# A transformer block on one NeuronCore: Q and K halves spilled head by head, each stack filled by one transfer

## What is computed

```python
x = x + attention(layernorm(x))     # x: 4 x 512 x 512, f32
x = x + ffn(layernorm(x))
# attention: 16 heads of 32, causal, softmax(q k^T / sqrt(32)) v, then @ Wo
# ffn: w1, w3 (1365 x 512) and w2 (512 x 1365), each rounded to -s, 0, +s
#      with s = mean |w|;  (silu(x w1^T) * (x w3^T)) w2^T
```

## Time and profile before

| | us |
|---|---|
| median of 3 runs | 585.4 |
| lowest and highest | 580.27, 587.4 |
| the profiled execution | 582.54 |
| its span in the profile | 580.8 |
| TensorE busy in that span | 544.1 (94%) |
| VectorE, GpSimd, ScalarE busy | 374.1, 290.1, 265.1 |

### The profile page before, as it was taken

The page is one execution under the profiler, slowest core; times in us unless marked ns, Lnnn a source line. Parts: engine busy times, 40 slices in busy tenths (PEclk is TensorE's granted clock), DMA queues, the critical chain, the costliest instruction groups (busy, mean ns, idle before and its releaser), DMA issues.

```text
span 580.8 us, 8895 instructions
## 1 busy us (share of the span) xinstructions
PE 544.1 (94%) x3148; PEld 250.3 (43%) x3148; DVE 374.1 (64%) x937; ACT 265.1 (46%) x437; POOL 290.1 (50%) x339
## 2 busy tenths in 40 slices
PE   3788888899879999999999999999989999999997
PEld 2343333344434444444444444444434444444443
DVE  7887787585998747545797666653865854554421
ACT  4867678656443455243244544422236654013320
POOL 5170598792763574811706662731537779113320
PEclk9898789999989999999999999999989999999999
DMA  8988848957563212203664003005430001150001
GB/s 323 322 173 236 211 113 230 232 148 184 92 137 98 59 35 75 56 2 105 151 146 127 3 19 91 1 19 165 114 70 0 2 2 46 46 126 1 0 19 54
DMA packets 82880, 58.52 MB, mean 101 GB/s; under 512 B 51434, under 2 KB 71914, under 8 KB 82836
## 3 DMA queue, kind: packets, MB, share of 16 engines
q1 hardware_dynamic: 82836, 57.95, 38.0%
HBM read 33.55 MB, written 12.58 MB: 79 GB/s over the span
## 4 chain that ended last, share of the span: by engine, by line
PE 73%; DVE 9%; POOL 8%; DMA 3%; ACT 3%; issue 2%; SPq 1%; DVEq 0%
PE work L1084 47%; PE work L1257 12%; PE prob_bank L1174 5%; PE score_bank L1152 4%; PE work L1195 4%; PE work L1217 2%; DVE masked L946 2%; POOL early L642 2%; ACT early L747 2%; DMA late<-rows 1%; POOL late L667 1%; POOL early L645 1%; POOL early L633 1%; DMA late<-in_L_attn_Wqkv 1%; DMA q_stack<-max_lo 1%
## 5 line engine op out<-in xcount | busy, mean ns | idle before, releaser
L1084 PE MATMUL work<-late,w_ternary 128*128 128x512 f16 (+1 forms) x704 | 160.3, 379 | 1.0 <-DMA late<-rows 1.0
L946 DVE CUSTOM_DVE_ANT_0 masked<-score_bank,mask 128x512 f16<-128x512 f32 (+3 forms) x256 | 111.8, 485 | 27.0 <-PE score_bank L1152 26.5
L747 ACT ACTIVATE early<-prob_bank,scalars 128x512 f32<-128x512 f32 x160 | 100.2, 682 | 61.8 <-PE prob_bank L1174 61.3
L1084 PEld LDWEIGHTS work<-late,w_ternary 128*128 128x128 f16 (+1 forms) x704 | 69.0, 100 | 77.4 <-issue 3.2
L633 POOL TENSOR_SCALAR_AFFINE_SELECT early<-early 128x640 f32<-128x640 f32 (+2 forms) x96 | 45.4, 506 | 78.2 <-ACT early L747 78.0
L659 POOL TENSOR_TENSOR late<-late 128x512 f16<-128x512 f32 (+1 forms) x44 | 50.9, 1159 | 61.6 <-ACT late L767 61.5
L1084 PE MATMUL work<-xt,wqkv_hi 128*128 128x512 f16 x256 | 78.6, 389 | 3.0 <-DVE wqkv_lo L901 3.0
L1257 PE MATMUL work<-w_ternary,late 128*128 128x512 f16 (+1 forms) x352 | 77.9, 379 | 0.0
L982 DVE SCALAR_TENSOR_TENSOR late<-late,work 128x512 f32<-128x512 f32 (+1 forms) x44 | 30.1, 685 | 53.0 <-ACT late L760 53.0
L767 ACT ACTIVATE late<-late 128x512 f16<-128x512 f32 (+1 forms) x44 | 27.7, 629 | 73.7 <-DVE late L993 73.7
L642 POOL TENSOR_TENSOR early<-early 128x768 f32<-128x768 f32 x32 | 58.1, 1815 | 2.5
(11 more groups left out here) (102 smaller groups left out, 689.9 us busy)
## 6 DMA issues: line engine op xcount, KB each, us to landing
rows<-in_L_attn_x SPq DMA_DIRECT2D x16, 256.0 KB, 2.9
q_stack<-q_hi_spill SPq DMA_DIRECT2D x32, 128.0 KB, 2.7
k_stack<-k_hi_spill SPq DMA_DIRECT2D x32, 128.0 KB, 3.0
x_res<-in_L_attn_x SPq DMA_DIRECT2D x12, 256.0 KB, 3.1
out_y<-x_res SPq DMA_DIRECT2D x12, 256.0 KB, 2.1
late<-in_L_ffn_w SPq DMA_DIRECT2D x4, 682.5 KB, 4.0
early<-in_L_ffn_w SPq DMA_DIRECT2D x3, 768.0 KB, 12.5
late<-in_L_ffn_w SPq DMA_DIRECT2D x3, 768.0 KB, 5.1
```

The costliest lines, as they stand in the source:

```text
L747: act.activation(probs[:, u, :], prob_bank[u % 2][:], ACT.Exp, scale=scalar(exp_scale)).then_inc(prob_free, 1)
L946: dve.tensor_tensor_reduce(masked[:, k % 2, 0:n], score_bank[u % 2][:, off:off + n], mask[:, S - n:S], 1.0, LOWEST, ALU.add, ALU.max, row_ ...
L1084: last = pe.matmul(bank, lhs, rhs, start=(n == 0), stop=(n == len(terms) - 1))
```

## The change

`spill_halves` writes three transfers instead of two for each of Q and K, the high half twice, into a DRAM tensor that has the heads outermost and the three parts of a stack inside each head. The high half goes out when ScalarE has made it, without waiting for the low one. `stack` then takes one transfer of 96 rows for each stack instead of three of 32. The semaphores `spilled` and `stacked` count accordingly. All five lists in `ORDERS` are laid anew; every step is still in them once.

```diff
-        spill = {key: nc.dram_tensor("_".join(key) + "_spill", [SLOTS, P, S], F16, kind="Internal").ap() for key in half}
+
+        spill = {n: nc.dram_tensor(f"{n}_spill", [SLOTS, HG, 3, HD, S], F16, kind="Internal").ap() for n in "qk"}
...
                 n, s = step
-                emptied(sp, step)
                 for part_ in ("hi", "lo"):
-                    sp.dma_start(spill[n, part_][s], half[n, part_][:]).then_inc(spilled[n, part_], 16)
+                    if part_ == "hi":
+                        sp.wait_ge(half_done, HALF[step] + 1)
+                    else:
+                        emptied(sp, step)
+                    for j in [j for j, at in enumerate(STACK_ROWS[n]) if at == part_]:
+                        sp.dma_start(spill[n][s, :, j], half[n, part_][:]).then_inc(spilled[n], 16)
...
                 for n, stacks in (("q", q_stack), ("k", k_stack)):
-                    for part_ in ("hi", "lo"):
-                        sp.wait_ge(spilled[n, part_], 16 * (s + 1))
-                        for j in [j for j, at in enumerate(STACK_ROWS[n]) if at == part_]:
-                            sp.dma_start(stacks[s % STACKS][j * HD:(j + 1) * HD, :, :],
-                                         spill[n, part_][s].rearrange("(h d) s -> d h s", h=HG)).then_inc(stacked[n][s % STACKS], 16)
+                    sp.wait_ge(spilled[n], 16 * 3 * (s + 1))
+                    sp.dma_start(stacks[s % STACKS][0:3 * HD, :, :],
+                                 spill[n][s].rearrange("h j d s -> (j d) h s")).then_inc(stacked[n][s % STACKS], 16)
...
                 if s:
-                    for part_ in ("hi", "lo"):
-                        act.wait_ge(spilled[n, part_], 16 * s)
+                    act.wait_ge(spilled[n], 16 * 3 * s)
...
-                        pe.wait_ge(stacked[n][s % STACKS], 16 * 3 * (s // STACKS + 1))
+                        pe.wait_ge(stacked[n][s % STACKS], 16 * (s // STACKS + 1))
```

Of the lists, the line of TensorE's that holds the first `probs`:

```diff
-        scores:0,3 v:0,2 scores:0,4 q:3 max_row:0 scores:1,0 k:3 probs:0,0 scores:1,1 v:0,3
+        scores:0,3 v:0,2 scores:0,4 q:3 max_row:0 scores:1,0 v:0,3 k:3 probs:0,0 scores:1,1
```

More of the change, by code:

```diff
@@ L94 @@
[L94 to L98, removed]
@@ L114 @@
[L114 to L117, removed]
+        stats_x:0,0 probs:0,0 unit:0-1 stats_x:0,1-3 weight_round:w1,0 probs:0,1 weight_round:w1,1-10
@@ L149 @@
+        gate:3,9 lin:3,9 gate:3,10 lin:3,10
     """,
     "dve": """
[L151 to L159, removed]
-        project:0,1 scores:6,1 stats_x:2,2-3 yt:0,0 scores:6,2 project:0,2 stats_y:0,1 xt:2,2 project:0,3
@@ L186 @@
+        project:3,3 norm_y:3,2 stats_y:3,3 yt:3,2 norm_y:3,3 yt:3,3 down:2,2-3 gate:3,0 lin:3,0 gate:3,1 lin:3,1
+        gate:3,2 lin:3,2 gate:3,3 lin:3,3 gate:3,4 lin:3,4 gate:3,5 lin:3,5 gate:3,6 lin:3,6 gate:3,7 lin:3,7
+        gate:3,8 lin:3,8 gate:3,9 lin:3,9 gate:3,10 lin:3,10 down:3,0-3
     """,
     "pe": """
-        xt:0,0-3 top_turn:qk q:0 k:0 top_turn:v weight_mean:w1 q:1 k:1 v:0,0 scores:0,0 v:0,1 scores:0,1 q:2
-        scores:0,2 top_turn:wo k:2 scores:0,3 v:0,2 scores:0,4 q:3 max_row:0 scores:1,0 k:3 probs:0,0 scores:1,1
@@ L220 @@
-        values:15 lin:2,10 sums:15 down:2,0-1 project:3,0-3 down:2,2-3 gate:3,0 lin:3,0 gate:3,1 lin:3,1
-        gate:3,2 lin:3,2 gate:3,3 lin:3,3 gate:3,4 lin:3,4 gate:3,5 lin:3,5 gate:3,6 lin:3,6 gate:3,7 lin:3,7
-        gate:3,8 lin:3,8 gate:3,9 lin:3,9 gate:3,10 lin:3,10 down:3,0-3
+        xt:0,0-3 top_turn:qk q:0 top_turn:v k:0 weight_mean:w1 q:1 k:1 v:0,0 scores:0,0 v:0,1 top_turn:wo
+        scores:0,1 q:2 scores:0,2 k:2 scores:0,3 v:0,2 scores:0,4 q:3 max_row:0 scores:1,0 v:0,3 k:3 probs:0,0
@@ new lines @@
+        max_row:4 scores:5,0 values:3 scores:5,1 sums:3 probs:4,0 scores:5,2 k:7 v:1,0 scores:5,3 probs:4,1
+        v:1,1 scores:5,4 v:1,2 max_row:5 v:1,3 project:0,0 probs:4,2 scores:6,0 project:0,1 probs:4,3 scores:6,1
+        project:0,2 probs:4,4 scores:6,2 project:0,3 scores:6,3 values:4 sums:4 probs:5,0 scores:6,4 probs:5,1
+        q:8 probs:5,2 k:8 probs:5,3 max_row:6 scores:7,0 q:9 scores:7,1 probs:5,4 gate:0,0 scores:7,2 lin:0,0
+        gate:0,1 scores:7,3 lin:0,1 scores:7,4 gate:0,2 max_row:7 lin:0,2 values:5 sums:5 probs:6,0 gate:0,3
@@ new lines @@
+        down:0,1 project:1,0 scores:10,2 down:0,2 project:1,1 down:0,3 scores:10,3 project:1,2-3 values:8 sums:8
+        probs:9,0 scores:10,4 q:12 probs:9,1 k:12 probs:9,2 max_row:10 q:13 scores:11,0 probs:9,3 gate:1,0
+        probs:9,4 lin:1,0 scores:11,1 gate:1,1 lin:1,1 scores:11,2 gate:1,2 lin:1,2 values:9 scores:11,3 sums:9
+        probs:10,0 q:14 gate:1,3 lin:1,3 scores:11,4 probs:10,1 k:13 max_row:11 probs:10,2 gate:1,4 probs:10,3
+        scores:12,0 k:14 probs:10,4 lin:1,4 scores:12,1 gate:1,5 scores:12,2 lin:1,5 gate:1,6 values:10
@@ new lines @@
+        scores:12,3 sums:10 probs:11,0 scores:12,4 lin:1,6 probs:11,1 q:15 gate:1,7 lin:1,7 gate:1,8 lin:1,8
+        probs:11,2 max_row:12 scores:13,0 k:15 probs:11,3 scores:13,1 gate:1,9 scores:13,2 probs:11,4 lin:1,9
+        gate:1,10 scores:13,3 lin:1,10 values:11 scores:13,4 down:1,0 sums:11 probs:12,0 down:1,1 max_row:13
+        scores:14,0 probs:12,1 down:1,2 scores:14,1 project:2,0 scores:14,2 probs:12,2 project:2,1 scores:14,3
+        probs:12,3 down:1,3 scores:14,4 project:2,2 v:3,0 probs:12,4 max_row:14 project:2,3 v:3,1-3 scores:15,0
@@ L405, in build @@
         out_stored = [sem(f"out_stored{i}") for i in range(ST)]
-        spilled = {key: sem("_".join(key) + "_spilled") for key in half}
+        spilled = {n: sem(f"{n}_spilled") for n in "qk"}
         stacked = {n: [sem(f"{n}_stacked{i}") for i in range(STACKS)] for n in "qk"}
```

203 lines of the change are left out of this document (102 added, 101 removed).

## The result

The changed kernel takes 621.9 us (median of 6 runs, 618.6 to 624.3) where the kernel before takes 582.6 in the same runs (6 runs, 580.3 to 587.4): a ratio of 1.067, 95% interval 1.064 to 1.070. The loss is 39 us. The forecast was 602, slower, with a range up to 618: the right side, and only half of the loss.

The account below looks back on a forecast made before the run. Matmuls were taken to bound 174 to 406 us, with DMA transfers competing in the first quarter. The sum 582.5 + 10 + 12 - 4.1 + 1.6 gave 602 us; own range 595 to 612, eight-in-ten range 572 to 618.

Parts of the forecast that it names:

- Four engines: Spills: four-block destinations use four DMA engines, 1.6 us per spill instead of 0.4, 8.0 us more per slot.
- First 98 us, +10: Start of the kernel: late K stack and late row maxima leave it 10 us late at 98, between 4 and 14.
- its transfers stand behind the spills of slot 2 and start some 2 later: `max_row:0` in the first 98 us: 8.0 us more on four engines; first `probs` moves by 10 to about 65.
- a queue on which TensorE does not wait: SyncE's issue queue: fewer issues might free 0.9 us per slot there, without gain to TensorE.
- The 0 for the issues: SyncE's issuing of spills and stacks, ten per slot becoming eight: counted 0, between -0.9 and +1.
- 98 to 145 us, +12: Slots 5 to 7 add 24 us, making 59 on four engines in a stretch of 47: 12 late.
- 174 to 406 us hidden: Full-clock matmul stretch: four engines carry 129 of 232 us, so the slower spills cost nothing.
- -4.1 around 426: Before `max_row:14`: the new order covers TensorE's waits and low clock, saving 4.1 us, between -5 and 0.
- Clock, +1.6: New waits of TensorE at the start lower its clock, costing 1.6 us.
- The large stack transfer and the doubled high half: Per slot: two stack transfers instead of six, hidden, 0; two more spills, 0.8 us of every engine if all sixteen share.
- Sixteen engines for 574: Rival: spills still spread over sixteen engines and the order brings gains of 3, 2 and 4 us; chance 0.29.
- Four engines bind throughout the start, 618: Rival: the whole 36 us of the check over 0 to 145 us is paid; chance 0.10.

Follow-up runs that it names:

- e1: The changed kernel with the spill tensor's three parts innermost, so a spill's destination has outer count 128 again; 582.7 us, ratio 1.001 to before.
- e9: The changed kernel with four-block spills in slots 0 to 3 only, e1's spills in all others; 601.1 us, ratio 1.033 to before.
- e12: The kernel before with each half spilled by four transfers of 32 rows instead of one of 128; 605.8 us, ratio 1.042.
- e10: The changed kernel with four-block spills in slots 4 to 7 only, e1's spills in all others; 591.7 us, ratio 1.017 to before.
- e11: The changed kernel with four-block spills in slots 8 to 15 only, e1's spills in all others; 590.9 us, ratio 1.016 to before.
- e2: The kernel before with the changed kernel's five lists and no other edit; 582.0 us, ratio 0.998.
- e14: e1 with `stack:15` moved ahead of `yt:2,1-2` in SyncE's list; 580.5 us, ratio 0.996 to before.
- e4: e1 with the lists of the kernel before; 584.3 us, ratio 1.002 to before.

## Why the prediction was right or wrong

The forecast's 19.5 us (10 + 12 - 4.1 + 1.6) met 39. In its own terms: the first 98 us were 9.5 short, 98 to 145 was 1.9 too much, and what lies after 145 came out at +9.3 instead of -4.1, which is the larger miss. The three measured parts are by slots and hold their own cost of clock, so they match the forecast's stretches only roughly.

**Four engines: right.** The term that was to decide did. A slot's six spills take what 6 x 1.6 us says, windows with spills alone show a quarter of the engines busy, and e1 takes the loss away with the shape alone.

**First 98 us, +10: undersized, 19.5 by e9.** The first link held: `scores:0,0` at 38.97 after a wait of 4.94 (forecast 37.5 and 4.5). The step that failed is "its transfers stand behind the spills of slot 2 and start some 2 later". It counted the DMA engines' queue and left out SyncE's: `max_lo` was issued 12.0 us later (63.39 for 51.42), 5.4 of them after the row maxima were turned. Ahead of it in the list the two turns of w1 held SyncE 5.5 us longer than before, the spills of slots 1 and 2 7.6 longer and the loads of w3 1.8; the stack's fewer issues and the pauses that SyncE had before gave only part of it back. So the first `probs` came at 70.28 and not near 65. The late queue also issued the weights of w3 late, for whose sum TensorE waited 5.19 at 88.24, a wait that no step of mine had. That SyncE's time is paid for at the end, e12 shows without any slow engine: "a queue on which TensorE does not wait" was wrong. The 0 for the issues, fewer but dearer, holds by the medians alone: 6 x 0.56 + 2 x 0.48 = 4.3 us per slot, as much as the ten before, 4 x 0.4 and 6 x 0.45. In the first slots single spills took SyncE up to 2.2 us to issue, 5.6 and 5.0 us for the six of slots 1 and 2, and that is where it counted. e1's six of each took 2.6.

**98 to 145 us, +12: right in size.** Slots 4 to 7 cost 10.1 (e10).

**174 to 406 us hidden, and -4.1 around 426: wrong, +9.3 by e11.** The sum of busy time (129 of 232 us) was no argument. A stack waits for the last of its own spills, 1.6 us for each one that four engines have ahead of it, however idle the others are. Where the list leaves less than that before the first `scores`, TensorE stands: 2.2 us at slot 8, where K's stack goes out at 224.91, 8.5 us after the first spill of `k:8`. At slot 15 it stands 5.4, by a longer way: the load behind the spill, VectorE, and `yt:2,2` ahead of the stack in SyncE's list. The gap before `max_row:14` did go, as forecast, but the new order as a whole brought about 1 us (e2), not the 4.1: it put `k:15` close ahead of the turns of y and `stack:15` behind them. I had named SyncE as what might give the gain back, but at `yt:2,3` behind `max_row:14`, not at `yt:2,1-2` ahead of the stack. Even with sixteen engines the wait there is 1.5 us, and e14 takes it out.

**Clock, +1.6: undersized.** Slower matmuls make 8.9 us of the longer span. From 70 to 88 us the mean granted clock is 0.50 (a window of the changed kernel), the lower level of 1.2 GHz, and most groups of three `scores` or `probs` take 1.01 to 1.06 us, where others take 0.60 at 2.4 GHz; ahead of them is the wait of 8.02. More waits, more low clock.

**The large stack transfer and the doubled high half, 0 and 0.8 us per slot hidden: right.** e4 has both and is 0.2% over before (interval 0.0 to 0.5%).

**Rivals.** Sixteen engines for 574 was a sum of gains that e1 and e2 don't show; such a kernel ties with before. "Four engines bind throughout the start, 618" came nearest in size, but by luck: it had 36 for the start and nothing later, and slots 0 to 7 cost 29.6, with a quarter of the loss in slots 8 to 15. Whether the four engines were full throughout the start no view shows; the share is a mean over all sixteen (0.64 from 98 to 145). What can be read is that SyncE's queue had no pause over 0.11 us from 35.50 to 67.9.

**Readings.** "The largest single wait ... 9.6 us" is the sum of two; the longest is 6.4. The 0.38 us of a matmul at full clock is right, but rows 7 don't show it. Neither enters the sum.

## What to carry to other kernels

Look at the outer counts of both sides of a transfer before its bytes. A scratch tensor can be laid so that a fuller load and a spread spill go together: with the parts innermost the same merge cost nothing. And when a transfer gets slower, ask not only who waits for it, but what else is queued on its engines and which issuing queue is held by that: turns of w1 held SyncE for 3.8 to 6.7 us each, and everything behind them in the list. In a list worked through in order, a step that still waits for another engine is as good as a slow transfer: moving one stack ahead of such a step gave 7.8 us. And a row of a timeline that joins several issues is no duration; look at them one by one before you give it a cause. Last, an average share of 0.28 hides nothing for a consumer that waits for the last of a burst; measure the burst against the gap the order leaves it.

## What the runs showed of the hardware that was not expected

The ten turns of weights, DMA transposes, hold SyncE 22.1 us in all before, 47.3 in the changed kernel and 25.7 in e1 (sums over the timelines); the longest single ones are 3.8, 6.7 and 7.1. So long holds are many with the four-engine spills, though e1 has one too, behind two loads of w2. It is not so for every transpose: `yt:2,1`, issued 0.6 us after the spill of `k:15` and one load, took 1.53 us, where such transposes elsewhere take 1.2 to 1.3. What in it waits was not tried apart. Plain transfers can hold SyncE as well: a spill took up to 2.2 us to issue, by the median 0.56.

The cost of fewer engines rises faster than their load (19, 39, 84 us for 6.4, 9.6 and 12.8 us per slot, with some 8 of the 84 due to more issues by estimate). Issues are dear by number, not size: 32 rows cost SyncE 0.42 to 0.45 us as 128 do, and 12 more per slot cost the kernel 24 us, where moving its spills from sixteen engines to four cost 19. And a destination in blocks costs 0.53 to 0.61 us to issue instead of 0.33 to 0.43, by the medians of SyncE's spills after and before.
